# Four graph layers with ReLU, split products and attention: a new order of layers and engines

## The reference

```python
    h = jnp.maximum(_layernorm(x, axis=-1), 0.0)
    x = x + _L0_gnn_ref(h, adj, L0_gnn_W, L0_gnn_a)
    ...   # the same line of h before each of the next three
    x = x + _L1_gnn_ref(h, adj, L1_gnn_kernel, L1_gnn_bias)
    x = x + _L2_gnn_ref(h, adj, L2_gnn_kernel)
    x = x + _L3_gnn_ref(h, adj, L3_gnn_W)
# layer 0: attention over nodes, masked where adj <= 0.5
    e = jax.nn.leaky_relu(Wh1 + jnp.swapaxes(Wh2, 1, 2), negative_slope=ALPHA)
    attention = jax.nn.softmax(jnp.where(adjacent_matrix > 0.5, e, NEG_INF), axis=1)
    return jax.nn.elu(jnp.einsum('bst,bto->bso', attention, Wh))
# layer 1: adjacency plus identity, scaled by degree ** -0.5 on both sides
    out = jnp.einsum('bnm,bmf,fc->bnc', An, X, kernel) + bias     # then relu
# layer 2
    out = jnp.einsum('bnf,fd->bnd', jnp.einsum('bnm,bmf->bnf', a, x), kernel)   # then relu, row mask
# layer 3
    agg = jnp.einsum('bij,bjf->bif', adj, x) / jnp.maximum(deg, EPS)
    out = jnp.einsum('bnf,of->bno', jnp.concatenate([x, agg], axis=2), W)       # then relu
```

## Time and profile before

| | us |
|---|---|
| median of 3 runs | 2874.55 (2872.74 to 2878.08) |
| span of the profiled execution | 2872.2 |
| VectorE busy in it | 2520.1 |
| ScalarE busy in it | 1092.3 |
| GpSimd busy in it | 1184.6 |

### The profile page before, as it was taken

The page is one execution under the profiler, slowest core; times in us unless marked ns, Lnnn a source line. Parts: engine busy times, 40 slices in busy tenths (PEclk is TensorE's granted clock), DMA queues, the critical chain, the costliest instruction groups (busy, mean ns, idle before and its releaser), DMA issues. The chain is left out here.

```text
span 2872.2 us, 46921 instructions
## 1 busy us (share of the span) xinstructions
PE 2646.5 (92%) x14600; PEld 2284.7 (80%) x14600; DVE 2520.1 (88%) x5467; ACT 1092.3 (38%) x2187; POOL 1184.6 (41%) x1287
## 2 busy tenths in 40 slices
PE   3799999998999999999998999989999998999988
PEld 2678788787888878788787887878888787887877
DVE  6888989898898989989889898988989889898974
ACT  2443434333343433433433443333334433343332
POOL 2443434444344443444434444443444434444331
PEclk8899999999999999999999999999999999999999
DMA  3111101011010111101111011010101111011000
GB/s 121 38 38 34 45 27 48 27 41 45 27 48 27 41 37 34 45 31 38 37 34 45 27 48 34 34 45 27 48 27 41 38 38 41 31 38 37 30 16 23
DMA packets 72865, 109.70 MB, mean 38 GB/s; under 512 B 4288, under 2 KB 37056, under 8 KB 72640
## 3 DMA queue, kind: packets, MB, share of 16 engines
q1 hardware_dynamic: 72640, 106.71, 11.2%
HBM read 73.14 MB, written 33.55 MB: 37 GB/s over the span
## 5 line engine op out<-in xcount | busy, mean ns | idle before, releaser
L808 POOL TENSOR_TENSOR h_lo<-h,h_hi 128x512 fp32r<-128x512 f32 x512 | 712.1, 1401 | 596.9 <-DVE h_hi L571 538.6
L330 PE MATMUL O<-w_hi,t_hi 128*128 128x512 f32 x2048 | 800.2, 391 | 1.4 <-DVE t_lo L647 1.2
L330 PE MATMUL O<-w_lo,t_hi 128*128 128x512 f32 x2048 | 798.4, 390 | 0.0
L330 PE MATMUL O<-w_hi,t_lo 128*128 128x512 f32 x2048 | 798.1, 390 | 0.0
L330 PE MATMUL T<-a_hi,h_hi 128*128 128x256 f32 x1536 | 463.5, 302 | 98.3 <-DVE t_lo L647 76.5
L571 DVE CAST h_hi<-h 128x512 fp32r<-128x512 f32 x512 | 332.1, 669 | 215.2 <-ACT h L520 215.0
L330 PEld LDWEIGHTS O<-w_hi,t_lo 128*128 128x128 f32 x2048 | 384.4, 188 | 81.8
L330 PE MATMUL T<-a_hi,h_lo 128*128 128x256 f32 x1536 | 446.2, 291 | 0.0
L330 PEld LDWEIGHTS O<-w_hi,t_hi 128*128 128x128 f32 x2048 | 386.4, 189 | 74.2 <-issue 2.6
L330 PE MATMUL T<-a_lo,h_hi 128*128 128x256 f32 x1536 | 445.2, 290 | 0.0
L330 PEld LDWEIGHTS O<-w_lo,t_hi 128*128 128x128 f32 x2048 | 385.8, 188 | 71.2
(11 more groups left out here) (83 smaller groups left out, 4291.5 us busy)
## 6 DMA issues: line engine op xcount, KB each, us to landing
x_in<-x SPq DMA_DIRECT2D x64, 512.0 KB, 3.3
out<-act_out SPq DMA_DIRECT2D x64, 512.0 KB, 2.8
a_raw<-adj_t SPq DMA_DIRECT2D x64, 256.0 KB, 2.8
a_rows<-adj SPq DMA_DIRECT2D x64, 256.0 KB, 2.7
xs<-w_all SPq DMA_DIRECT2D x7, 512.0 KB, 4.8
t_mean<-w_all SPq DMA_DIRECT2D x3, 512.0 KB, 4.5
v_rows<-a_vecs SPq DMA_DIRECT2D x1, 512.0 KB, 5.4
bias_rows<-bias SPq DMA_DIRECT2D x1, 256.0 KB, 8.3
```

What stands on the lines that cost most here:

```text
L330: last = nc.tensor.matmul(psum, s, m, start=(start and n == 0 and i == 0), stop=(stop and n == len(pairs) - 1 and i == 2))
L808: nc.gpsimd.tensor_tensor(h_lo[:, b, m], h[:, b, m], h_hi[:, b, m].bitcast(F32), ALU.subtract).then_inc(h_lo_ready, 1)
```

## The change

Graphs follow each other four periods apart and the layers of one graph five apart, so a period's layer is j mod 4 and every fourth period is the same (`Plan`). All periods are written out; there is no loop and no register arithmetic. A graph's x lies in one of six buffers from its load to its store, and x_in is gone.

In layer 3 the weights come first: TensorE multiplies the transposed h by the fifth weights into T (`project_first`), T is split as in the other layers, and then the adjacency gathers it into O with 512 columns per matmul, 12 in all (`gather_last`). The product of h with the fourth weights goes to X, ScalarE copies it to z (`own_term`), and VectorE takes O times the reciprocal degree plus z, then ReLU and the add in one pass of 1024 elements (`mean_relu`). t_mean and recip_rows are gone, and h is split into h_hi and h_lo in layers 0 to 2 only. The weights are split in the order 0, 1, 2, 4, 3.

h_hi is cast by ScalarE in one instruction of 1024 elements. The leaky ReLU of the scores is an activation on ScalarE ahead of the exp; VectorE finds the row maximum in the same pass that adds the mask (L567) and computes the shift from it. Layer 2's add to xs, the row mask and the variance's epsilon are on GpSimd. Layer 1's ReLU and add are one pass of 1024 elements. Inside a period, VectorE does t_lo straight after finishing the last step (and after the softmax, in the period that has one) and leaves the statistics to the end; statistics are made four periods ahead (five for layer 0), h and its parts three (h of layer 0 four).

```diff
-STREAMS = 4
+SPACING = 5
...
+WEIGHT_ORDER = (0, 1, 2, 4, 3)
+X_BUFS = 6
+A_BUFS = 4
...
+    def position(self, graph, layer):
+        return LAYERS * graph + SPACING * layer
+
+    def graph(self, k):
+        return (k - SPACING * (k % LAYERS)) // LAYERS
...
+            def t_free(k, b):
+                wait(pe, t_lo_ready, k.part(ALL, NT, b, back=1))
...
+            def project_first(k):
+                if k.g == 0:
+                    wait(pe, w_lo_ready, 2 * WEIGHT_ORDER.index(4) + 2)
+                wait(pe, ht_lo_ready, k.done(L3, NT))
+                for n in range(NT):
+                    t_free(k, n)
+                    h_times(k, flat(T[:, HALF * n:HALF * n + HALF]), n, 4).then_inc(t_ready, 1)
...
-                        parts = [(ht_hi[:, f, c], ht_lo[:, f, c], w_hi[:, 3, f], w_lo[:, 3, f]) for f in range(FT)]
-                        last = product(O[:, k.odd, n], parts, start=False)
...
-            for step in periods(pe):
-                if step(2).layer in (0, 3):
-                    spread(step(2))
-                if step(1).valid:
-                    gather(step(1))
-                if step(0).valid:
-                    project(step(0))
-                if step(1).layer == 3:
-                    transpose_h(step(1), 1)
...
+            def gather_last(k):
+                if k.g == 0:
+                    wait(pe, w_lo_ready, 2 * WEIGHT_ORDER.index(3) + 2)
+                wait(pe, scores_ready, k.done(L0, NT, back=-1))
+                for n in range(NT):
+                    h_times(k, X[:, n], n, 3).then_inc(z_psum_ready, 1)
+                for n in range(NT):
+                    c = slice(n * P, n * P + P)
+                    o_free(pe, k, n)
+                    parts = []
+                    for m in range(NT):
+                        wait(pe, t_lo_ready, k.part(ALL, NT, m))
+                        u = slice(HALF * m, HALF * m + HALF)
+                        parts.append((a_hi[:, k.ab, m, c], a_lo[:, k.ab, m, c], flat(t_hi[:, k.odd, u]), flat(t_lo[:, k.odd, u])))
+                    product(O[:, k.odd, n], parts).then_inc(o_ready, 1)
+
+            for j in slots:
+                if step(j + 2).layer == 0:
+                    spread(step(j + 2))
+                if step(j + 1).layer in L012:
+                    gather(step(j + 1))
+                if step(j + 1).layer == 3:
+                    project_first(step(j + 1))
+                if step(j + 2).layer == 3:
+                    transpose_h(step(j + 2))
+                if step(j).layer in L012:
+                    project(step(j))
+                if step(j).layer == 3:
+                    gather_last(step(j))
...
+            def high_part(k):
+                wait(act, h_ready, k.done(ALL, NT))
+                wait(act, t_ready, k.done(ALL, NT, back=2))
+                nc.scalar.copy(h_hi[:, k.odd], h[:, k.odd]).then_inc(h_hi_ready, 1)
...
+            def own_term(k):
+                wait(act, out_ready, k.done(L3, back=4))
+                for n in range(NT):
+                    wait(act, z_psum_ready, k.part(L3, NT, n))
+                    nc.scalar.copy(z[:, n], X[:, n]).then_inc(z_ready, 1)
...
-                for m in range(NT):
+                wait(act, neg_ready, k.done(L0))
+                for m in range(NT):
+                    nc.scalar.activation(scores[:, m], scores[:, m], ACT.Prelu, bias=wh[:, k.g % 2, 1, m:m + 1],
+                                         alpha=SLOPE).then_inc(leaky_ready, 1)
+                for m in range(NT):
+                    wait(act, leaky_ready, k.part(L0, NT, m))
                     nc.scalar.activation(scores[:, m], scores[:, m], ACT.Exp, bias=s_neg[:, m:m + 1],
                                          accum_out=s_sum[:, m:m + 1]).then_inc(exp_ready, 1)
...
-            for step in periods(act):
-                if step(2).layer == 3:
-                    spread_recip(step(2))
-                if step(2).layer in (1, 2, 3):
-                    activate(step(2))
-                if step(-1).valid:
-                    finish(step(-1))
-                if step(2).layer == 0:
-                    exps(step(2))
-                if step(3).layer == 0:
-                    activate(step(3))
-                if step(1).valid:
-                    gather(step(1))
-                if step(1).layer == 3:
-                    transposed(step(1), 1)
-                if step(3).valid:
-                    prepare(step(3))
-                if step.half is not None:
-                    split_weight(step.half)
...
+            for j in slots:
+                if step(j - 1).layer == 0:
+                    elu(step(j - 1))
+                if step(j - 1).layer == 2:
+                    masked_relu(step(j - 1))
+                if step(j + 3).layer in (1, 3):
+                    activate(step(j + 3))
+                if step(j + 2).layer == 0:
+                    exps(step(j + 2))
+                if step(j + 1).layer is not None:
+                    gathered(step(j + 1), 0)
+                if step(j + 3).layer == 1:
+                    high_part(step(j + 3))
+                if step(j + 1).layer is not None:
+                    gathered(step(j + 1), 1)
+                if step(j + 4).layer == 0:
+                    activate(step(j + 4))
+                if step(j + 5).layer == 1:
+                    with_self(step(j + 5))
+                if step(j + 3).layer == 0:
+                    high_part(step(j + 3))
+                if step(j + 2).layer == 3:
+                    transposed(step(j + 2))
+                if step(j + 3).layer == 2:
+                    activate(step(j + 3))
+                    high_part(step(j + 3))
+                    without_self(step(j + 3))
+                if step(j).layer == 3:
+                    own_term(step(j))
+                for i in halves_at.get(j, ()):
+                    split_weight(i)
...
+                    nc.vector.scalar_tensor_tensor(act_out[:, 1, n], O[:, k.odd, n], deg_rsqrt[:, k.xb, n:n + 1],
+                                                   bias_rows[:], ALU.mult, ALU.add).then_inc(psum_taken, 1)
+                wait(dve, psum_taken, k.done(L013, NT))
+                nc.vector.scalar_tensor_tensor(flat(xs[:, k.xb]), flat(act_out[:, 1]), 0.0, flat(xs[:, k.xb]), ALU.max,
+                                               ALU.add).then_inc(l1_done, 1)
+
...
+            def mean_relu(k):
+                for n in range(NT):
+                    wait(dve, z_ready, k.part(L3, NT, n))
+                    wait(dve, o_ready, k.part(ALL, NT, n))
+                    nc.vector.scalar_tensor_tensor(z[:, n], O[:, k.odd, n], deg_recip[:, k.xb, n:n + 1], z[:, n],
+                                                   ALU.mult, ALU.add).then_inc(psum_taken, 1)
+                wait(dve, psum_taken, k.done(L013, NT))
+                nc.vector.scalar_tensor_tensor(flat(xs[:, k.xb]), flat(z[:]), 0.0, flat(xs[:, k.xb]), ALU.max,
+                                               ALU.add).then_inc(out_ready, 1)
...
-                if step(2).layer in (1, 2, 3):
-                    high_part(step(2))
-                if step(-1).valid:
-                    finish(step(-1))
-                if step(3).layer in (2, 3):
-                    statistics(step(3))
-                if step(2).layer == 0:
-                    softmax_parts(step(2))
-                if step(3).layer == 0:
-                    dots(step(3))
-                if step(1).valid:
-                    gather(step(1))
-                if step(3).layer == 0:
-                    high_part(step(3))
-                    add_mask(step(3))
-                if step(3).layer == 1:
-                    statistics(step(3))
-                if step(2).layer == 2:
-                    mask_rows(step(2))
-                if step(1).layer == 3:
-                    transposed(step(1), 1)
-                if step(2).layer == 0:
-                    degrees(step(2))
-                if step(3).valid:
-                    prepare(step(3))
-                if step.half is not None:
-                    split_weight(step.half)
+                if step(j + 2).layer == 0:
+                    mask_scores(step(j + 2))
+                if step(j - 1).layer == 3:
+                    mean_relu(step(j - 1))
+                if step(j - 1).layer == 0:
+                    positive_part(step(j - 1))
+                if step(j - 1).layer == 1:
+                    scaled_relu(step(j - 1))
+                if step(j + 1).layer == 0:
+                    degrees(step(j + 1))
+                if step(j + 2).layer == 0:
+                    softmax_parts(step(j + 2))
+                if step(j + 1).layer is not None:
+                    gathered(step(j + 1), 0)
+                    gathered(step(j + 1), 1)
+                if step(j + 5).layer == 1:
+                    with_self(step(j + 5))
+                if step(j + 4).layer == 0:
+                    dots(step(j + 4))
```

(17 more changed lines are left out.)

790 lines of the change are left out of this document (343 added, 447 removed).

## The result

The kernel after takes **2654.11 us** (median of four runs, 2653.33 to 2654.37). Beside it, the kernel before took 2875.09 (2872.74 to 2878.08). The ratio is 0.9232, 95% interval 0.9221 to 0.9244. The forecast was 2660, range 2625 to 2745. The profiled execution spans 2652.4 us.

The account below looks back on a forecast made before the run. It took TensorE as bound, losing 182 us mid-run waiting on a full, badly ordered VectorE. Clean work 2574 + start 64 + middle 8 + end 12 = 2658 us of span, forecast 2660, range 2625 to 2745.

Parts of the forecast that it names:

- Clean work: TensorE's own matmuls and transposes without waits: 40.2 us a graph, 2574 us for 64 graphs.
- the 1% on top: Allowance on TensorE's counted work, from its longest nearly idle-free stretch: 39.83 becomes 40.2 us a graph.
- matmuls of 512 columns still 0.228 apart: Sign in the profile after: TensorE's 512-column pace unchanged; a gather slower than 0.228 us would make the forecast wrong.
- Middle: TensorE's loss between start and end of the run: 8 us instead of 182, since no period makes it wait.
- Start: TensorE's loss before it becomes continuous near 117 us: 64 us, as before, bounds 45 to 90.
- End: TensorE's loss at the last graph, its chain sticking out and last passes and store: 12 us, 8 to 20.
- The walk of four periods: Each engine's queue followed through one graph's periods; tightest in layer 2's, t_lo at 25.7, due 28.9, 3.2 us spare.
- The wait is VectorE's fullness and order: Cause given for TensorE's waits for t_lo and the middle's 182 us: not a transfer, not TensorE's own work.
- (2): Rival: one wait a graph stays, likely t_lo behind layer 2's softmax, passes stretching beside GpSimd; 2735 to 2800 us; chance 0.13.
- (3): Rival: slower than before, VectorE stretched throughout, both two-input passes of 1024 included; 2965 us at 8 more; chance 0.03.
- break-even: Where the slower rival matches the time before: 3.3 us of stall a graph, needing 6.5 us more in the chain.
- (4): Rival: only the start is worse, weight splits in VectorE's queue delaying TensorE a whole graph, 40 us: 2700; chance 0.12.

Follow-up runs that it names:

- b2: Kernel before, loop written out, with t_lo and t_mean ahead of statistics, softmax and dots on VectorE: 2904.18 us, ratio 1.0097.
- a3: Kernel after with the statistics of the coming layers put back ahead of t_lo, all offloads kept: 2656.98 us, ratio 0.9239.
- b3: Kernel before, loop written out, with h_hi cast on ScalarE right behind the activation: 2809.17 us, ratio 0.9772.
- a2: Kernel after with the h_hi cast and layer 2's add back on VectorE: 2651.4 us, ratio 0.922.
- a4: Kernel after with statistics, normalisation, activation, dots and layers 1 and 2's h_hi and h_lo one period later: 2941.1 us, ratio 1.0232.
- a5: Kernel after with five useless VectorE passes ahead of the softmax in every layer-2 period: 2708.8 us, ratio 0.9424.
- a6: Kernel after with nine useless VectorE passes ahead of the softmax in every layer-2 period: 3013.3 us, ratio 1.0481.
- the grid: Matmuls alone, no graph computed, against neither kernel, with stationary and moving tiles shifted by 0 to 480 bytes: for example 12 matmuls in 2.73 us, then 2.79.
- a8: Kernel after with three unused tiles (64, 192, 192 bytes) and the second graph's exps and two w_lo reordered at the start: 2620.33 us, ratio 0.9107.

## Why the prediction came out, step by step

**The sum.** Forecast 2574 + 64 + 8 + 12 = 2658 of span; measured 2566 (64 x 40.10) + 73 + 1 + 12 = 2652.
- *Clean work*, 40.2 a graph against 40.10. The value held, by luck, for the terms did not: in the chain, by which the forecast counted too, 132 matmuls of 512 columns cost 0.6 us more (5.60 + 4 x 5.58 + 2.77 = 30.69 for 30.06), the 72 of 256 0.3 less (8.33 for 8.67), the transposes the same (1.09 for 1.10), and the 1% on top, 0.4, was not there. Half of that 1% was in truth the kernel before's slow gathers: 0.123 for the 72 from a, where I had taken 0.1204 from one piece of the chain. I took TensorE's pace for a constant of the shape; it goes with the layout, which the change moved (it added buffers ahead of t). I had named "matmuls of 512 columns still 0.228 apart" as a sign and the contrary as what would make the forecast wrong: by that sign the forecast was wrong, at a price of some 40 us (64 x 0.63), and the total was rescued by terms of the other sign.
- *Middle*, 8 against 1.4 (2360 less 12587/214 x 40.10), or 1 in the sum. Right.
- *Start*, 64 against 73, within its bounds. It is what is left of the 86 us besides clean work; 61.7 of it is idle, 17.0 and 9.4 behind p_lo of the second and third graph, the rest the slower clock. TensorE was continuous from 136 us, not 117.
- *End*, 12 against 12: 4.2 idle behind ht_lo, 5.5 behind the last matmul, some 2 of clock.

**The engines.** VectorE 29 forecast, 28.1 measured; ScalarE 22 and 21.9; GpSimd 19.5 and 18.6; p_hi took 0.351 us in the median, forecast near 0.34. The walk of four periods hit its tightest place within 0.1 us, but by luck: the softmax was 1.1 us earlier than walked, and a wait for t_hi of 1.2 us, behind the cast h_hi on ScalarE, which the walk did not have, made up for it.

**The cause.** "The wait is VectorE's fullness and order" is the step that failed, though its number held. t_lo ahead of everything, the softmax included, made it worse (b2), and statistics ahead of t_lo cost nothing in the kernel after (a3). The cast taken off VectorE gave 66 us (b3), and undoing most of the offload cost nothing (a2). Undoing the extra period between h and its gather cost 287 (a4). The reading that fits all five: in the kernel before VectorE was late because it stood in its queue waiting for h, 215 us of it, in a chain through GpSimd and ScalarE that had one period too few; t_lo, behind it in the queue, was where TensorE saw it. The row of that wait stands in the earlier trace rows, and the prediction makes no use of it. The change did all three things, so the forecast could not tell them apart. Open stays what the extra period alone, or the change's order alone, would do in the kernel before, and what load and order undone together would do in the kernel after: no run shows it.

**The rivals.** (2) didn't come, but a5 shows that its mechanism lay 3.6 us away: p_hi slid beside GpSimd, as its condition said. The trace before bears out its premise: from 300 to 2700 us, 28 p_hi passes ran with no GpSimd pass of over 1 us beside them and took 0.352 us in the median, the other 82 took 1.10. In the kernel after none of the 128 ran beside one. (3)'s evidence was read wrongly: that L604 kept to 677 to 742 ns says nothing, since passes with two SBUF inputs stretch up to 2.4 times in a6; in the whole trace before, none of L604's 128 passes overlapped a GpSimd pass of over 1 us by more than 0.2 us. L598's, which did, took 1.77 us in the median. The earlier trace rows had only lengths, and I said myself that they didn't show this. Its break-even of 6.5 us more in the chain is too high: 6.2 us of passes gave 139 us above the kernel before, because the stretch (2.2) and the clock (1.6) come on top. (4) was a matter of 9 us.

**Open.** Why the kernel after's gathers from a ran at 0.114 when the grid gives 0.118 for the difference 64, and when a8 with the same residues also ran at 0.118; and why the kernel before's ran at 0.123 where the grid gives 0.120. By what mechanism the difference of addresses acts, no run shows.

## What to carry to other kernels

When an engine is late with what the bound engine waits for, look first at what it waited for itself: its longest own wait can name a chain that is short of a period, and here the lead there was needed where load taken off it was not. Count room not only to the due time but to the moment at which a pass slides beside another engine's. And a tile added or removed moves all tiles behind it: compare the matmuls' distance before and after a change as a term of its own, and try a small unused tile.
